# Cross attention's product of probabilities and values: four column positions of 32 x 64 in place of two of 64 x 128

## The chip, the core and the metric

The kernel runs on one core of one Trainium2 chip. The core has TensorE (PE, matmuls), VectorE (DVE), ScalarE (ACT), GpSimd (POOL) and SyncE (SP, which issues the loads here). Each engine works through its own list of instructions and waits on semaphores for the others. What is measured is the device time of one launch in microseconds (us).

## What is computed

One block of a Perceiver: cross attention of 8 x 64 tokens on a context of 8 x 512 rows, a linear attention, and a mixture of 16 experts with a shared expert, each with a layer norm and a residual. The change touches the first of them:

```python
def _L0_xattn_ref(q, k, v, Wq, bq, Wk, bk, Wv, bv, Wo, bo):
    qh = (q @ Wq + bq).reshape(b, n, H, HD)
    kh = (k @ Wk + bk).reshape(b, k.shape[1], H, HD)
    vh = (v @ Wv + bv).reshape(b, v.shape[1], H, HD)
    scores = jnp.einsum('blhe,bshe->bhls', qh, kh)
    attn = jax.nn.softmax(scale * scores, axis=-1)
    out = jnp.einsum('bhls,bshd->blhd', attn, vh)
    out = out.reshape(b, n, H * HD)
    return out @ Wo + bo
...
x = x + _L0_xattn_ref(_layernorm(x, axis=-1), ctx_1024, ctx_1024, ...)
```

For each of the 8 batches and each of the 16 heads, 64 x 512 probabilities are multiplied by 512 x 32 values; the 16 results of 32 columns stand side by side as the 512 rows of the output projection.

## The kernel before

All of it is one program with an order written out by hand. Activations stand transposed (features on partitions). `P` is 128, `B` = 8 batches, `L` = 64 tokens, `HD` = 32, `KT` = `NS` = 4 tiles of 128, `HPT` = 4 heads in a tile, `PAIRS` = 8 pairs of heads. `ps` is PSUM, eight banks of 128 partitions x 512; the bank `AV` (4) takes the attention's output.

The cross attention runs over the batches. PE's step for batch b is `step(b, par)`: keys of b for three tiles (`project_k`, L964), transposes of the first tile of probabilities of batch b-1 (`probs_transpose`, L1037), keys of the last tile, `attention(b-1)`, and then `values_and_scores(b)`: scores of the first two tiles (`score_group`, L1010), two tiles of values (L964), scores of the other two tiles, two tiles of values. After the seventh step `attention(7)` follows alone, and then the output projection (`residual`, L1093), which waits for `o_done`.

`attention(b)` is `probs_transpose(1)`, `attend(0)`, `probs_transpose(2)`, `attend(1)`, `probs_transpose(3)`, `attend(2)`, `attend(3)`. A `probs_transpose(ht)` turns the 512 probabilities of two pairs of heads into two PSUM banks; ACT copies the first (L469), DVE the second (L702), to `probs_T`, and `attend(ht)` waits for both copies (`pT_done`). The next transposes wait for the copies too, since they write the same two banks.

A pair of heads shares 128 rows of `probs`, and so 128 columns of `probs_T`: 64 tokens of one head on one side and 64 of the other on the other side; which head stands on which side alternates with the tile. `attend` (L1047) takes the value columns of both heads of a pair (64) as weights and all 128 columns of `probs_T` as the moving operand. Half of the 64 x 128 result is what is wanted, each head's values by its own tokens, and the other half, each head's values by the other's tokens, is left in the bank. The two pairs of a tile go to the lower and the upper 64 partitions (two column positions of the array).

`o_out` (L710, DVE) picks the wanted blocks out of the bank, for each head of a tile by itself (32 partitions, four blocks of 64), adds the bias of the values and writes `o_T`, whose rows are those of the output projection. It waits for all four attends of a batch (`o_ps`).

DVE's step is: four copies of transposed probabilities (L702), `o_out(b-1)`, `ctx_low(b+1)` (L680, the low part of the next context; it needs ACT's `ctx_high`, L442), and `softmax(b)` (maxima L727, reciprocals L717, scaling L719). ACT's step is: the bias of the keys (L458), its copies of probabilities (L469), `ctx_high(b+1)`, and the exponentials of the scores (L476) with the copies of the values between (L454). PE's second group of scores waits for the third exponential of the first group. In step 7 there is no next context, and `ctx_high` and `ctx_low` are left out.

Matmuls of type fp32 are carried out as two instructions each; a program's list shows one, the trace two.

Of the kernel before, what the change touches and what calls it, by code (L numbers as in the profile page):

```python
# [16 lines left out]
ALU = mybir.AluOpType  # L17
# [3 lines left out]
P = 128  # L21
B, L, S, D = 8, 64, 512, 512
H, HD, FEAT = 16, 32, 128
# [3 lines left out]
KT = D // P  # L27
NS = S // P
NF = FF // P
HPT = P // HD  # L30
# [8 lines left out]
def perceiver_block(nc, x_d, ctx_d, wq_d, bq_d, wk_d, bk_d, wv_d, bv_d, wo_d, bo_d, wqkv_d, proj_d,  # L39
                    wout_d, bout_d, gate_d, wg_d, wu_d, wd_d, wsg_d, wsu_d, wsd_d, out_d):  # L40
    main = ExitStack()
    with main:
# [44 lines left out]
        v_s = sb(cross, "v_s", [P, NS, D])  # L87
# [8 lines left out]
        probs_T = sb(cross, "probs_T", [P, 2, 2, NS, P])  # L96
        o_T = sb(cross, "o_T", [P, KT, TOK])
# [5 lines left out]
        bias_v = sb(cross, "bias_v", [P, KT])  # L103
# [16 lines left out]
        rows = ExitStack()  # L120
# [85 lines left out]
        ps = main.enter_context(nc.psum_tensor("ps", [P, 8, BANK], F32))  # L206

        def bank(n):
            return ps[:, n, :]
# [21 lines left out]
        o_ps, o_done = sem("o_ps"), sem("o_done")  # L231
# [25 lines left out]
        PROJ, TRANS, AV = (0, 1), (2, 3), 4  # L257
# [374 lines left out]
        def _(dve):  # L632
# [71 lines left out]
            def o_out(b):  # L704

                dve.wait_ge(o_ps, b * KT + KT)
                for hh in range(HPT):
                    rows = slice(HD * hh, HD * (hh + 1))
                    blocks = slice(1, 3) if hh % 2 else slice(0, 4, 3)
                    dve.tensor_tensor(o_T[rows, :, bass.ds(b * L, L)].rearrange("p (t u) l -> p t u l", u=2),  # L710
                                      bank(AV).rearrange("p (t c l) -> p t c l", t=2, l=L)[rows, :, blocks, :],
                                      bias_v[rows, :].rearrange("p (t u) -> p t u", u=2).unsqueeze(3).to_broadcast(
                                          [HD, 2, 2, L]), ALU.add).then_inc(o_done, 1)

            def normalise(b, p):
                dve.wait_ge(exp_done, b * PAIRS + p + 1)
# [84 lines left out]
            u = w = a = 0  # L801
            for kind, i, r in LIN_ORDER:
# [24 lines left out]
                else:  # L827
# [4 lines left out]
                    for par in range(2):  # L832
                        ins = dve.tensor_scalar(den[L * par:L * (par + 1), a, :].rearrange("p (k h) -> p k h", k=2),
                                                got[par][:, :, :, HD], 1e-8, None, ALU.add)
                    link(ins)
                    link(dve.reciprocal(den_inv[:, a, :], den[:, a, :]))
                    for par in range(2):
                        rows = slice(L * par, L * (par + 1))
                        ins = dve.tensor_tensor(att[rows, r, 256 * i:256 * (i + 1)].rearrange("p (k h c) -> p k h c", k=2, h=HPT),
                                                got[par][:, :, :, 0:HD],  # L840
                                                den_inv[rows, a, :].rearrange("p (k h) -> p k h", k=2).unsqueeze(3).to_broadcast(
                                                    [L, 2, HPT, HD]), ALU.mult)
# [45 lines left out]
            for b in range(B):  # L888
                ins = dve.max(top_w[:, b, :], score_T[:, L * b:L * (b + 1)])
            link(ins)  # L890
            for b in range(B):
                ins = dve.max_index(top_i[:, b, :], top_w[:, b, :], score_T[:, L * b:L * (b + 1)])
# [13 lines left out]
            for i in range(2):  # L906
                dve.wait_ge(pick_ps, i + 1)
                cols = slice(BANK * i, BANK * (i + 1))
# [40 lines left out]
        def _(pe):  # L949
# [91 lines left out]
            def attend(b, ht):  # L1041
                for pr in range(2):
                    pe.wait_ge(pT_done[pr], b * KT + ht + 1)
                for st in range(NS):
                    for pr in range(2):
                        cols = slice(2 * HD * (2 * ht + pr), 2 * HD * (2 * ht + pr + 1))
                        ins = pe.matmul(ps[64 * pr:64 * (pr + 1), AV, P * ht:P * (ht + 1)], v_s[:, st, cols],  # L1047
                                        probs_T[:, ht % 2, pr, st, :], start=(st == 0), stop=(st == NS - 1),
                                        skip_group_check=True)
                ins.then_inc(o_ps, 1)  # L1050

            def attention(b):
# [16 lines left out]
            for ht in range(KT):  # L1069
                cols = slice(P * ht, P * (ht + 1))  # L1070
                for dt in range(KT):
                    for i, (w, c) in enumerate(((wq_hi, xn_hi), (wq_hi, xn_lo_cross), (wq_lo, xn_hi))):
                        ins = pe.matmul(bank(2 + ht), w[:, dt, cols], c[:, dt, :],  # L1073
                                        start=(dt == 0 and i == 0), stop=(dt == KT - 1 and i == 2))
# [19 lines left out]
                                        start=(dt == 0), stop=(dt == KT - 1))  # L1094
                    ins.then_inc(res_ps, 1)

            pe.wait_ge(o_done, B * HPT)
            pe.wait_ge(wo_in, 16)
            residual(0, o_T, w_o)

# [32 lines left out]
            u = w = a = 0  # L1133
            for kind, i, r in LIN_ORDER:
                if kind == "p":
                    qkv_project(i)
                elif kind in "kq":
# [6 lines left out]
                    if kind == "k":  # L1144
                        for pr in range(2):
                            for part in range(2):
                                ins = pe.matmul(ps[:, u % 3, 2 * FEAT * pr:2 * FEAT * (pr + 1)],
                                                kl_halves[:, i, pr, P * r:P * (r + 1)],
                                                proj_parts[part][:, 2 * i + pr].rearrange("p h f -> p (h f)"),
                                                start=(part == 0), stop=(part == 1))  # L1150
                    else:
                        for part in range(2):
                            ins = pe.matmul(bank(u % 3), proj_parts[part][:, 2 * i + r // 2, r % 2, :],
                                            ql_halves[:, i, r // 2, :], start=(part == 0), stop=(part == 1))
# [14 lines left out]
                else:  # L1169
# [5 lines left out]
                    for h in range(2 * HPT):  # L1175
                        ins = pe.matmul(ps[:, 3 + 2 * (a % 2) + h // HPT, 2 * KVW * (h % HPT):2 * KVW * (h % HPT + 1)],  # L1176
                                        q_feat[:, 8 * i + h, P * r:P * (r + 1)], kv[:, r, 8 * i + h, :],
                                        start=True, stop=True)
# [189 lines left out]
```

## Time and profile before

| what | value |
|---|---|
| timed runs (3) | median 737.51 us, 737.16 to 739.67 |
| profiled execution | 737.64 us |
| its span on the core | 735.9 us |
| mean granted TensorE clock | 0.99 of 2.4 GHz |
| PE busy | 685.9 us, 93% |
| PE weight loads (beside matmuls) | 440.2 us, 60% |
| DVE busy | 302.4 us, 41% |
| ACT busy | 239.7 us, 33% |
| POOL busy | 42.5 us, 6% |
| L1047, matmuls of `attend` | 512 instructions, 33.8 us busy |
| L1037, transposes of probabilities | 256 instructions, 34.1 us busy |
| start of the output projection of the cross attention | 300.1 us of the span |

A span is the time from the first to the last instruction of the program on the core; what lies around it is in the execution's time alone. Busy time of an engine is the time in which at least one of its instructions is under way, so that matmuls that overlap are counted once, while the mean ns of one is its whole length, the way through the array included. An engine's time matters where the others wait for it. The rows further down show this for one step of the cross attention.

### The profile page before, as it was taken

Reading aid. Unit: us, or ns where it says so; the run is one execution under the profiler, and the core shown is the slowest. Engines: PE = TensorE matmul, PEld = TensorE weight load, DVE = VectorE, ACT = ScalarE, POOL = GpSimd, SP = SyncE. Lnnn points to the kernel's source line nnn. Section 1 sums busy time; section 2 is a strip of 40 time slices with the busy share of each in tenths; the row PEclk is TensorE's granted clock in tenths of the full one; section 3 lists DMA queues with packets and bytes.
Section 4 is the critical chain, followed back from the end, with each engine's and each line's share of the span. In section 5 each row is a group of like instructions: output and inputs, shape, how many; then the busy total and the mean of one; then the engine's idle time right before and its main releaser. Section 6 shows DMA issues by size and latency. Waiting matters only on the chain.

```text
span 735.9 us, 9457 instructions
## 1 busy us (share of the span) xinstructions
PE 685.9 (93%) x3760; PEld 440.2 (60%) x3760; DVE 302.4 (41%) x619; ACT 239.7 (33%) x468; POOL 42.5 (6%) x43
## 2 busy tenths in 40 slices
PE   6699999999999999869998989999999999999996
PEld 5468687877768687447897565344444444444532
DVE  4844726445362717576678654111111111111112
ACT  4444434354443525144675122111111111111110
POOL 0800000000000000065000010000000000000000
PEclk9999999999999999989999999999999999999999
DMA  8110101011033000030209740799999999999921
GB/s 302 55 58 1 58 2 57 1 58 55 4 136 151 1 1 1 1 100 24 102 16 419 280 201 1 264 348 376 407 366 412 355 405 356 384 377 380 391 81 60
DMA packets 14344, 129.63 MB, mean 176 GB/s; under 512 B 2720, under 2 KB 2848, under 8 KB 6240
## 3 DMA queue, kind: packets, MB, share of 16 engines
q1 hardware_dynamic: 12384, 127.09, 44.7%
q10 hardware_dynamic: 1920, 1.97, 0.9%
q8 instruction: 30, 0.49, 0.3%
q14 instruction: 10, 0.08, 0.0%
HBM read 126.03 MB, written 1.05 MB: 173 GB/s over the span
## 4 chain that ended last, share of the span: by engine, by line
PE 77%; DVE 13%; ACT 4%; issue 3%; DMA 1%; SPq 1%; ACTq 1%; DVEq 0%
PE ps L964 17%; PE ps L1206 14%; PE ps L1238 8%; PE ps L1213 7%; PE ps L1047 4%; PE ps L1245 4%; PE ps L1127 4%; PE ps L1037 4%; DVE ctx_lo L680 2%; PE ps L1227 2%; PE ps L1164 2%; PE ps L1073 2%; PE ps L1010 1%; PE ps L1176 1%; DVE neg_max L727 1%
## 5 line engine op out<-in xcount | busy, mean ns | idle before, releaser
L860 DVE TENSOR_TENSOR hid<-hid,ps 128x256 f32<-128x256 f32 (+1 forms) x32 | 17.6, 553 | 141.6 <-PE ps L1206 91.8
L702 DVE COPY probs_T<-ps 128x512 f32<-128x512 f32 x32 | 22.1, 692 | 99.9 <-PE ps L1037 99.9
L476 ACT ACTIVATE probs<-ps,neg_max 128x512 f32<-128x512 f32 x64 | 43.8, 687 | 57.1 <-DVE neg_max L727 57.1
L585 ACT ACTIVATE hid<-ps 128x256 f32<-128x256 f32 (+1 forms) x32 | 15.7, 490 | 141.6 <-PE ps L1213 86.5
L1238 PE MATMUL ps<-w_d,hid_T 128*64 128x512 f32 x256 | 58.4, 598 | 1.4 <-ACT hid_T L600 1.4
L1206 PE MATMUL ps<-w_u,x_slot 128*64 128x512 f32 x256 | 58.4, 598 | 0.0
L1206 PE MATMUL ps<-w_g,x_slot 128*64 128x512 f32 x256 | 57.8, 593 | 0.0
L964 PE MATMUL ps<-wv_hi,ctx_hi 128*128 128x512 f32 x128 | 52.5, 410 | 4.1 <-POOL wv_lo L395 4.1
L964 PE MATMUL ps<-wv_lo,ctx_hi 128*128 128x512 f32 x128 | 50.5, 395 | 0.0
L964 PE MATMUL ps<-wv_hi,ctx_lo 128*128 128x512 f32 x128 | 50.5, 394 | 0.0
L964 PE MATMUL ps<-ctx_hi,wk_hi 128*128 128x512 f32 x112 | 44.5, 398 | 0.0
L964 PE MATMUL ps<-ctx_hi,wk_lo 128*128 128x512 f32 x112 | 43.8, 391 | 0.0
L727 DVE TENSOR_REDUCE neg_max<-ps 128x1 f32<-128x512 f32 x64 | 42.5, 684 | 3.2 <-PE ps L1010 3.0
L964 PE MATMUL ps<-ctx_lo,wk_hi 128*128 128x512 f32 x112 | 43.6, 389 | 0.0
L458 ACT ACTIVATE k_T<-ps,bias_k 128x512 f32<-128x512 f32 x32 | 21.8, 688 | 57.0 <-PE ps L964 57.0
L1206 PEld LDWEIGHTS ps<-w_g,x_slot 128*64 128x64 f32 x256 | 18.1, 137 | 37.1 <-issue 37.1
L1238 PEld LDWEIGHTS ps<-w_d,hid_T 128*64 128x64 f32 x256 | 17.0, 136 | 34.1 <-issue 32.3
L964 PEld LDWEIGHTS ps<-wv_hi,ctx_hi 128*128 128x128 f32 x128 | 24.4, 191 | 21.3 <-issue 6.5
L1206 PEld LDWEIGHTS ps<-w_u,x_slot 128*64 128x64 f32 x256 | 17.1, 136 | 30.5 <-issue 30.5
L1037 PE MATMUL ps<-ident,probs 128*128 128x128 f32 x256 | 34.1, 276 | 0.4 <-ACT probs_T L469 0.4
L1047 PE MATMUL ps<-probs_T,v_s 128*64 128x128 f32 x512 | 33.8, 278 | 0.0
L876 DVE TENSOR_TENSOR eo<-ps,eo 64x512 f32<-64x512 f32 x15 | 10.3, 688 | 56.8 <-ACT eo L612 56.8
(192 smaller groups left out, 1167.9 us busy)
## 6 DMA issues: line engine op xcount, KB each, us to landing
w_u<-in_wu SPq DMA_DIRECT2D x16, 2048.0 KB, 16.2
w_d<-in_wd SPq DMA_DIRECT2D x16, 2048.0 KB, 14.7
w_g<-in_wg SPq DMA_DIRECT2D x16, 2048.0 KB, 10.4
ctx_raw<-in_ctx SPq DMA_DIRECT2D x7, 1024.0 KB, 4.8
w_qkv<-in_wqkv SPq DMA_DIRECT2D x1, 3072.0 KB, 13.8
ws_g<-in_wsg SPq DMA_DIRECT2D x1, 2048.0 KB, 7.8
ws_u<-in_wsu SPq DMA_DIRECT2D x1, 2048.0 KB, 7.6
ws_d<-in_wsd SPq DMA_DIRECT2D x1, 2048.0 KB, 22.4
```

What stands on the lines that cost most here:

```text
L458: act.activation(k_T[:, ht, :], bank(FIRST_K + ht if first else PROJ[ht % 2]), ACT.Identity, bias=bias_k[:, ht:ht + 1], scale=1.0).then_in ...
L476: act.activation(probs[:, p, :], bank(SCORE[p]), ACT.Exp, bias=neg_max[:, p:p + 1], scale=1.0, accum_out=row_sum[:, p:p + 1]).then_inc(exp ...
L702: dve.tensor_copy(probs_T[:, ht % 2, 1].rearrange("p s c -> p (s c)"), bank(TRANS[1])).then_inc(pT_done[1], 1)
L727: dve.tensor_reduce(neg_max[:, p:p + 1], bank(SCORE[p]), AX.X, ALU.max, negate=True).then_inc(max_done, 1)
L964: ins = pe.matmul(dst, a(dt), c(dt), start=(dt == 0 and i == 0), stop=(dt == KT - 1 and i == 2))
L1037: ins = pe.transpose(ps[:, TRANS[pr], P * st:P * (st + 1)], probs[:, 2 * ht + pr, P * st:P * (st + 1)], ident[:])
L1047: ins = pe.matmul(ps[64 * pr:64 * (pr + 1), AV, P * ht:P * (ht + 1)], v_s[:, st, cols], probs_T[:, ht % 2, pr, st, :], start=(st == 0), st ...
L1127: ins = pe.matmul(bank(qkv_bank(n)), a, c, start=(dt == 0 and i == 0), stop=(dt == KT - 1 and i == 2))
L1206: ins = pe.matmul(ps[64 * fh:64 * (fh + 1), dst, :], x_slot[:, dt, e, :], weights[e % 2][:, dt, BANK * fh:BANK * (fh + 1)], start=(dt == 0 ...
L1213: ins = pe.matmul(ps[:, dst, 0:w], xn_T[:, dt, P * t:P * (t + 1)], shared[:, dt, f:f + w], start=(dt == 0), stop=(dt == KT - 1))
L1238: ins = pe.matmul(ps[64 * fh:64 * (fh + 1), 6 + n % 2, :], hid_T[:, n % 2, j, 64 * fh:64 * (fh + 1)], w_d[e % 2][:, KT * fh + j, :], start ...
L1245: ins = pe.matmul(bank(6 + n % 2), hid_T[:, n % 2, j, :], ws_d[:, ITEMS[n][2] // P + j, :], start=(j == 0), stop=(j == tiles - 1))
```

## The change

`attend` takes each head by itself. Its weights are the 32 value columns of one head, its moving operand the 64 columns of `probs_T` that are this head's tokens, and its result goes to the 32 partitions `HD * j` of the bank, in columns `L * ht`: four column positions, one for each head of a tile. Nothing is computed that isn't used; the number of multiplied blocks is halved and the number of matmuls doubled. The results of a batch fill half of the bank (256 columns), with rows and tiles as `o_T` has them, and `o_out` becomes one instruction over 128 partitions. PE's wait for `o_done` counts one for each batch.

```diff
--- before.py
+++ after.py
@@ -704,13 +704,9 @@
             def o_out(b):
 
                 dve.wait_ge(o_ps, b * KT + KT)
-                for hh in range(HPT):
-                    rows = slice(HD * hh, HD * (hh + 1))
-                    blocks = slice(1, 3) if hh % 2 else slice(0, 4, 3)
-                    dve.tensor_tensor(o_T[rows, :, bass.ds(b * L, L)].rearrange("p (t u) l -> p t u l", u=2),
-                                      bank(AV).rearrange("p (t c l) -> p t c l", t=2, l=L)[rows, :, blocks, :],
-                                      bias_v[rows, :].rearrange("p (t u) -> p t u", u=2).unsqueeze(3).to_broadcast(
-                                          [HD, 2, 2, L]), ALU.add).then_inc(o_done, 1)
+                dve.tensor_tensor(o_T[:, :, bass.ds(b * L, L)],
+                                  bank(AV)[:, 0:KT * L].rearrange("p (t l) -> p t l", l=L),
+                                  bias_v[:].unsqueeze(2).to_broadcast([P, KT, L]), ALU.add).then_inc(o_done, 1)
 
             def normalise(b, p):
                 dve.wait_ge(exp_done, b * PAIRS + p + 1)
@@ -1042,11 +1038,12 @@
                 for pr in range(2):
                     pe.wait_ge(pT_done[pr], b * KT + ht + 1)
                 for st in range(NS):
-                    for pr in range(2):
-                        cols = slice(2 * HD * (2 * ht + pr), 2 * HD * (2 * ht + pr + 1))
-                        ins = pe.matmul(ps[64 * pr:64 * (pr + 1), AV, P * ht:P * (ht + 1)], v_s[:, st, cols],
-                                        probs_T[:, ht % 2, pr, st, :], start=(st == 0), stop=(st == NS - 1),
-                                        skip_group_check=True)
+                    for j in range(HPT):
+                        pr, side = j // 2, (j + ht) % 2
+                        cols = slice(P * ht + HD * j, P * ht + HD * (j + 1))
+                        ins = pe.matmul(ps[HD * j:HD * (j + 1), AV, L * ht:L * (ht + 1)], v_s[:, st, cols],
+                                        probs_T[:, ht % 2, pr, st, L * side:L * (side + 1)],
+                                        start=(st == 0), stop=(st == NS - 1), skip_group_check=True)
                 ins.then_inc(o_ps, 1)
 
             def attention(b):
@@ -1094,7 +1091,7 @@
                                         start=(dt == 0), stop=(dt == KT - 1))
                     ins.then_inc(res_ps, 1)
 
-            pe.wait_ge(o_done, B * HPT)
+            pe.wait_ge(o_done, B)
             pe.wait_ge(wo_in, 16)
             residual(0, o_T, w_o)
```

On PE, in step 1, around `attention(0)`: `probs_T,v_s` are the matmuls of `attend`, `ident,probs` the transposes, `k_T,q_T` the scores. Before:

```order
L1037 MATMUL ps<-ident,probs 128x128 x8
L1047 MATMUL ps<-probs_T,v_s 64x128 x8
L1037 MATMUL ps<-ident,probs 128x128 x8
L1047 MATMUL ps<-probs_T,v_s 64x128 x8
L1037 MATMUL ps<-ident,probs 128x128 x8
L1047 MATMUL ps<-probs_T,v_s 64x128 x16
L1010 MATMUL ps<-k_T,q_T 64x512 x8
```

After:

```order
L1033 MATMUL ps<-ident,probs 128x128 x8
L1044 MATMUL ps<-probs_T,v_s 32x64 x16
L1033 MATMUL ps<-ident,probs 128x128 x8
L1044 MATMUL ps<-probs_T,v_s 32x64 x16
L1033 MATMUL ps<-ident,probs 128x128 x8
L1044 MATMUL ps<-probs_T,v_s 32x64 x32
L1006 MATMUL ps<-k_T,q_T 64x512 x8
```

The places stay; each block of attend has twice the matmuls, of a quarter of the size.

On DVE, in the loop over the steps, between the last copy of probabilities and the first maxima (ISA and REGISTER_ALU set registers for addresses and waits). Before:

```order
L702 COPY probs_T<-ps 128x512
L706 ISA
L710 ISA
L710 TENSOR_TENSOR o_T<-ps,bias_v 32x4x64
L710 ISA
L710 TENSOR_TENSOR o_T<-ps,bias_v 32x4x64
L710 ISA
L710 TENSOR_TENSOR o_T<-ps,bias_v 32x4x64
L710 ISA
L710 TENSOR_TENSOR o_T<-ps,bias_v 32x4x64
L679 REGISTER_ALU
L680 TENSOR_TENSOR ctx_lo<-ctx_raw,ctx_hi 128x2048
```

After:

```order
L702 COPY probs_T<-ps 128x512
L706 ISA
L707 ISA
L707 TENSOR_TENSOR o_T<-ps,bias_v 128x4x64
L679 REGISTER_ALU
L680 TENSOR_TENSOR ctx_lo<-ctx_raw,ctx_hi 128x2048
```

Three instructions and their address registers are gone; the order of the rest is the same.

## Rows read from the trace of the kernel before

**Rows 1.** The page's chain of work that ended last, shares of the span.
```profile
PE 77%; DVE 13%; ACT 4%; issue 3%; DMA 1%; SPq 1%; ACTq 1%; DVEq 0%
PE ps L964 17%; PE ps L1206 14%; PE ps L1238 8%; PE ps L1213 7%; PE ps L1047 4%; PE ps L1245 4%; PE ps L1127 4%; PE ps L1037 4%; DVE ctx_lo L680 2%; PE ps L1227 2%; PE ps L1164 2%; PE ps L1073 2%; PE ps L1010 1%; PE ps L1176 1%; DVE neg_max L727 1%
```

**Rows 2.** The page's costliest groups: busy us, mean ns, idle before.
```profile
L1047 PE MATMUL ps<-probs_T,v_s 128*64 128x128 f32 x512 | 33.8, 278 | 0.0
```

**Rows 3.** PE's waits over the span: us in total, times, longest.
```profile
PE ps L1010 <- ACT probs L476: 8.1, 6, 1.4
...
PE ps L1316 <- DMA eo_slot<-eo: 1.2, 1, 1.2
```

**Rows 4.** Timeline of a step, all engines: start us, us, engine, line.
```profile
64.05 1.03 PE L1037 MATMUL ps<-ident,probs 128*128 128x128 f32 x8
...
68.45 0.57 ACT L469 COPY probs_T<-ps 128x512 f32<-128x512 f32 x1
...
68.63 1.09 PE L1047 MATMUL ps<-probs_T,v_s 128*64 128x128 f32 x16
68.74 0.69 DVE L702 COPY probs_T<-ps 128x512 f32<-128x512 f32 x1 [2.92 <-PE ps L1037]
...
69.66 1.09 PE L1037 MATMUL ps<-ident,probs 128*128 128x128 f32 x8
...
72.73 2.04 PE L1047 MATMUL ps<-probs_T,v_s 128*64 128x128 f32 x32
72.83 0.69 DVE L702 COPY probs_T<-ps 128x512 f32<-128x512 f32 x1 [1.36 <-PE ps L1037]
72.88 1.90 ACT L442 CAST ctx_hi<-ctx_raw 128x2048 fp32r<-128x2048 f32 x1
...
74.70 1.11 PE L1010 MATMUL ps<-k_T,q_T 32*64 32x512 f32 x16
74.93 1.77 DVE L710 TENSOR_TENSOR o_T<-ps,bias_v 32x256 f32 x4 [1.40 <-PE ps L1047]
...
76.73 2.29 DVE L680 TENSOR_TENSOR ctx_lo<-ctx_raw,ctx_hi 128x2048 fp32r<-128x2048 f32 x1
...
82.50 0.19 ACT L476 ACTIVATION_READ_ACCUMULATOR probs<-ps,neg_max 128x1 f32 x1
...
82.81 0.27 PEld L1010 LDWEIGHTS ps<-k_T,q_T 32*64 32x64 f32 x16 [1.75 <-issue]
82.84 1.12 PE L1010 MATMUL ps<-k_T,q_T 32*64 32x512 f32 x16 [1.36 <-ACT probs L476]
```

**Rows 5.** Timeline of step 7, PE, the two groups of scores.
```profile
276.33 1.11 PE L1010 MATMUL ps<-k_T,q_T 32*64 32x512 f32 x16
...
283.04 1.11 PE L1010 MATMUL ps<-k_T,q_T 32*64 32x512 f32 x16
```

**Rows 6.** DVE's groups by shape: busy us, mean ns, idle before.
```profile
L710 DVE TENSOR_TENSOR o_T<-ps,bias_v 32x256 f32 x24 | 10.1, 421 | 8.9 <-PE ps L1047 8.4
...
L860 DVE TENSOR_TENSOR hid<-hid,ps 128x256 f32<-128x256 f32 x16 | 6.6, 419 | 43.9 <-PE ps L1213 43.9
```

**Rows 7.** Single lines: ns of one instruction, min/median/max.
```profile
L1010 PEld LDWEIGHTS ps<-k_T,q_T x256: 127/130/132, 47.7 to 283.1; 32*64 32x64 f32 x128
L1010 PE MATMUL ps<-k_T,q_T x256: 587/598/638, 47.8 to 283.6; 32*64 32x512 f32 x128
...
L1037 PE MATMUL ps<-ident,probs x256: 270/273/330, 64.1 to 296.0; 128*128 128x128 f32 x128
```

**Rows 8.** Timeline of PE, four heads' keys times values: 96 moving columns.
```profile
371.10 1.03 PE L1164 MATMUL ps<-v_bd,k_feat 128*128 128x96 f32 x8
```

**Rows 9.** Timeline of the last attention's end, DVE and PE.
```profile
298.30 1.77 DVE L710 TENSOR_TENSOR o_T<-ps,bias_v 32x256 f32<-32x256 f32 x4 [1.28 <-PE ps L1047]
...
300.13 3.27 PE L1093 MATMUL ps<-w_o,o_T 128*128 128x512 f32 x7 [1.87 <-DVE o_T L710]
```

**Rows 10.** One stretch: busy (count) of PE, PEld, DVE, ACT, POOL; clock, DMA.
```profile
67.60:82.80 15.20, 13.88 (x129) 10.61 (x127) 9.47 (x16) 6.46 (x12) 0.00 (x0) 1.00 0.16 56
```

## The prediction

> **What bounds the kernel now.** I read the page's chain first, then PE's waits, then the timeline of one batch step, then single lines for prices. The profiled execution took 737.64 us, its span is 735.9 us, and 1.7 us lie around it; the timed runs have a median of 737.51 us, so a sum made against the profile holds for the median within 0.13 us. TensorE (PE) carries 77% of the chain that ended last, VectorE (DVE) 13% [rows 1]. The changed matmuls (L1047) have 4% of it and keep PE busy for 33.8 us [rows 1, 2]. They all lie in the cross attention, which ends with o_T at 300 us [rows 9]; what follows can only be shifted. Loads won't undo the shift: the one wait of PE for a DMA takes 1.2 us and is for a transfer that the kernel itself makes late [rows 3], and the experts' loads are started by work that shifts along.
>
> Seven batch steps and a last attention make up the stage. A step shows three things [rows 4]. First, transposes (eight, L1037) and probabilities times values ("attend", sixteen TensorE instructions, L1047, since each fp32 matmul is carried out as two) take turns with no idle time: an attend from 68.63 to the transposes at 69.66, 1.03 us, and four such blocks up to 72.73. The last two attends stand together, and the scores follow at 74.70. Second, DVE turns to the attention's output only when the last attend has ended: o_T from 74.93 for 1.77 us, ctx_lo for 2.29 up to 79.02, then the row maxima. Third, PE needs exponentials that hang on those maxima and arrives too early: the second group of scores starts at 82.84 after 1.36 us idle. That wait occurs six times and sums to 8.1 us [rows 3]. In step 7, which has no ctx_lo, the way from the first group to the second takes 283.04 - 276.33 = 6.71 us [rows 5] where the others need 82.84 - 74.70 = 8.14 [rows 4]: the stall is worth 1.43 us. So a step has two bounds: PE to the end of attention, then DVE and ScalarE (ACT) up to the second group of scores. The granted clock is 1.00, the level of 2.4 GHz, over both parts, with the stall in it [rows 10]; I expect no change of it.
>
> **DVE: four instructions become one.** Each o_T instruction works on 32 partitions with 256 elements in each and takes 420 ns; the four last 1.77 us [rows 4, 6]. The new one has 128 partitions and the same 256 elements. A sum with a PSUM operand on 128 x 256 takes 419 ns [rows 6]: partitions cost nothing, elements do. I take 0.42 us, a gain of 1.77 - 0.42 = **1.35 us** a batch. The bound above is 1.77, if each group of partitions were paid for, and no gain; the row speaks against it. The wait on o_done counts one a batch in place of four, has the same last event and costs nothing.
>
> **PE: four column positions.** Before, an attend is eight rounds of two instructions, one for each half of the array's columns, with 64 weight columns and 128 tokens. Eight transposes, also with 128 moving columns, take 1.03 us, of which 0.27 are the last one's own: a round is (1.03 - 0.27)/7 = 0.109 us [rows 4, 7]. The attend's sixteen fit in about the same length, so its two halves run side by side and a round of two costs what one matmul costs. The block of 1.03 is 0.05 for the first weights, 7 x 0.109 = 0.76, and 0.21 up to the next block, where the engine changes its tiling.
>
> After, it is eight rounds of four, each with 32 weight columns and 64 moving columns. A round goes with the moving columns: seven instructions with 512 take 3.27 us, about (3.27 - 0.60)/6 = 0.445 us each with the first one's weights in it, four times the 0.109 of 128 [rows 7, 9]. Eight matmuls with 96 moving and 128 weight columns take 1.03 us, as long as transposes with 128 and 128: there the weights are the bound, at about 0.11 [rows 8]. So 32 weight columns cost about 0.027 and 64 moving columns 0.055, and a round costs **0.055 us** if four positions run together. No row shows four. The nearest are the scores (L1010), with eight positions, four of rows by two of columns, and 512 columns: sixteen instructions take 1.11 us, of which 0.59 are the last one's own, so all start within 0.52 us, where sixteen in a row would need some 7 [rows 4, 7, 9]. Nor is issuing the limit: their sixteen weight loads take 0.27 us, less 0.13 for the last, so they start within 0.14 with half of the matmuls between them, 24 instructions at 6 ns [rows 4, 7]. A round of four needs eight instructions, 0.05 us. That is nearly the round itself, so this cover is thin. The bounds: 0.055 by the columns from below, 0.22 from above if four positions take turns; 0.109 if a round keeps its price. I take 0.055, since the row nearest to it, the attend itself, pays nothing for its second column position. The new block: 0.03 + 7 x 0.055 + 0.02 + 0.20 = 0.64 us, **0.39 us** less.
>
> The Trainium skill has a rule against this. Its page "TensorE: Matmul & The Clock Gate", section "Wait — 56ns, not 53.3ns?", says that the starts of two matmuls are never less than some 25 ns apart, however small they are. By it a round of four takes 0.10 us, the attend gains 0.06, and the kernel ends at about 727 us (an estimate from the page's figure). The starts in the scores' rows, 6 ns an instruction, disagree with it where the positions differ.
>
> **What lies on the path.** Four attends a batch, but not each pays. The first two stand between transposes, and these wait for the copies of their banks. The ACT copy ends at 68.45 + 0.57 = 69.02, the DVE copy at 68.74 + 0.69 = 69.43; the next transposes would start at 69.66 - 0.39 = 69.27, and the half that needs the DVE copy about 0.5 us later [rows 4]. Both are in time; the next pair stands alike. The fourth needs the DVE copy of the last transposes, which ends at 72.83 + 0.69 = 73.52; with 0.15 us to be told (as from the third exponential's end at 82.69 to PE's 82.84) that is 73.67. Today the fourth starts at 74.70 - 1.03 = 73.67 [rows 4]. So the 0.39 us of the third turn into a wait for DVE, and the fourth pays again. Attention gains 3 x 0.39 = **1.17 us** a batch.
>
> Steps 1 to 6: PE gains 1.17 + 1.43 = 2.60 up to the second group of scores; the chain over DVE gains 1.17 + 1.35 = 2.52 and stays last by 0.08. What could be late next is ctx_hi, which ctx_lo needs: ACT ends it at 72.88 + 1.90 = 74.78 [rows 4], two attends earlier 74.00, and o_T then ends at 74.93 + 1.77 - 2.52 = 74.18: in time by 0.18. So six steps gain 6 x 2.52 = 15.1 us. Step 7 has no stall to lose: 1.17. The last attention gains 1.17, and PE stands idle through its o_T until 300.13 [rows 9], 1.35 more: 2.52. Sum 15.1 + 1.2 + 2.5 = **18.8 us**: 737.6 - 18.8 = 718.8 us.
>
> **Rivals.** (a) Issuing keeps a round at about 0.082 us, halfway: the attend gains 0.19, a step 0.57 + 1.35 = 1.92, in all 6 x 1.92 + 0.57 + 1.92 = 14.0, so 723.6 us. For it speaks the thin cover. (b) The PE part doesn't do what it says: each matmul keeps its price of 0.109/4 = 27 ns whatever its size, the round stays at 0.109, and DVE alone pays, 7 x 1.35 = 9.5 us: 728.1 us. Against it stand the 6 ns of the scores. The page's 25 ns comes out beside it. (c) Slower: the four positions take turns on the moving side, since four streams of tokens are read from the same 128 partitions, where the scores and the attend read two. A round is 4 x 0.055 = 0.22, an attend grows by 7 x 0.11 = 0.77 us, 32 of them by 24.6, less 9.5 of DVE: 752.7 us. It decides from a round of 0.109 + 9.5/(32 x 7) = 0.151 us, 38 ns a matmul. Against it: the second stream costs nothing today. (d) The third attend pays too: 8 x 0.39 = 3.1 more, 715.7 us. Its copy is tied to the transposes, so little speaks for it.
>
> **How the numbers follow.** Forecast, with (d) as its edge: 0.72; (a) 0.10; (b) 0.10; (c) 0.06; nothing that can be measured 0.02. The time is the forecast's. The range goes from (d), 715.5, to just beyond (a), 724.5; (b), (c) and no change are left out, 0.18. A measurement of this kernel tells about 0.5% (3.7 us) from no change: faster 0.92, same 0.02, slower 0.06.
>
> **What would show it.** L1047's successor should have 1024 instructions and some 21 us busy in place of 33.8; the starts of transposes should follow at 1.66 us in place of 2.05; PE should idle about 0.3 us before the fourth attend; o_T should be eight instructions of 0.42 us; PE's wait for the exponentials should fall from 8.1 us to under 1. I am wrong if an attend block takes over 0.8 us ((a) or (b)) or over 1.03 ((c)), or if ctx_lo starts late behind ctx_hi.

## The result, and the profile after

The changed kernel takes 717.06 us (median of four, 716.97 to 717.97) against 738.59 us of the kernel before in the same comparison (737.16 to 739.73): a ratio of 0.971, 95% interval 0.969 to 0.974. The forecast was 718.8, range 715.5 to 724.5. The profiled execution took 717.97 us, with a span of 716.2 us.

The page's line on the chain that ended last, which answers [rows 1]:

```profile
PE 82%; DVE 10%; ACT 3%; DMA 1%; issue 1%; SPq 1%; ACTq 1%; DVEq 0%
```

The group of the new matmuls among PE's lines (busy us, mean ns of one, idle before them), which answers [rows 2]:

```profile
L1044 PE MATMUL ps<-probs_T,v_s 128*32 128x64 f32 x1024 | 20.9, 222 | 2.3 <-DVE probs_T L702 2.3
```

The product has twice its instructions and 20.9 us busy in place of 33.8. PE's share of the chain rose, DVE's fell. PE's waits, which answer [rows 3] (us in total, times, longest):

```profile
PE ps L1044 <- DVE probs_T L702: 2.3, 8, 0.3
```

The wait for the exponentials is gone from the list; in its place stands one for the copies of the probabilities, eight times 0.29 us. The same step as in [rows 4] (timeline: start us, us, engine, line):

```profile
68.16 0.58 ACT L469 COPY probs_T<-ps 128x512 f32<-128x512 f32 x1
...
68.34 0.65 PE L1044 MATMUL ps<-probs_T,v_s 128*32 128x64 f32 x32
...
68.92 1.09 PE L1033 MATMUL ps<-ident,probs 128*128 128x128 f32 x8
...
71.55 0.65 PE L1044 MATMUL ps<-probs_T,v_s 128*32 128x64 f32 x32
71.66 0.69 DVE L702 COPY probs_T<-ps 128x512 f32<-128x512 f32 x1 [0.91 <-PE ps L1033]
71.70 1.90 ACT L442 CAST ctx_hi<-ctx_raw 128x2048 fp32r<-128x2048 f32 x1
...
72.50 0.65 PE L1044 MATMUL ps<-probs_T,v_s 128*32 128x64 f32 x32 [0.29 <-DVE probs_T L702]
...
73.08 1.11 PE L1006 MATMUL ps<-k_T,q_T 32*64 32x512 f32 x16
73.33 0.42 DVE L707 TENSOR_TENSOR o_T<-ps,bias_v 128x256 f32 x1 [0.98 <-PE ps L1044]
73.67 2.28 DVE L680 TENSOR_TENSOR ctx_lo<-ctx_raw,ctx_hi 128x2048 fp32r<-128x2048 f32 x1
...
79.30 0.19 ACT L476 ACTIVATION_READ_ACCUMULATOR probs<-ps,neg_max 128x1 f32 x1
...
79.80 1.11 PE L1006 MATMUL ps<-k_T,q_T 32*64 32x512 f32 x16
```

An attend has 0.65 us from its first start to its last end, and its block, from 68.34 to the transposes at 68.92, is 0.58 us where it was 1.03. The first two give what they save. The third starts at 71.55, the fourth only at 72.50, since DVE's copy (71.66 + 0.69) has to end first. o_T is one instruction of 0.42 us. The second group of scores starts 79.80 - 73.08 = 6.72 us after the first, as step 7 did all along; it was 8.14. The rest of the step is unchanged, so one step takes 108.32 - 74.70 = 33.6 us before and 103.91 - 73.08 = 30.8 us after. The next step's first scores in the timeline of before:

```profile
108.32 1.11 PE L1010 MATMUL ps<-k_T,q_T 32*64 32x512 f32 x16
```

and in the timeline of after:

```profile
103.91 1.11 PE L1006 MATMUL ps<-k_T,q_T 32*64 32x512 f32 x16
```

And the end of the last attention, which answers [rows 9]:

```profile
278.76 0.42 DVE L707 TENSOR_TENSOR o_T<-ps,bias_v 128x256 f32<-128x256 f32 x1 [0.86 <-PE ps L1044]
...
279.24 3.27 PE L1090 MATMUL ps<-w_o,o_T 128*128 128x512 f32 x7 [0.54 <-DVE o_T L707]
```

From the first scores to the output projection PE takes 300.13 - 47.78 = 252.35 us before and 279.24 - 47.50 = 231.74 after: **20.6 us** less, all of it in the stretch the prediction spoke of. The profiled pair differs by only 19.7 us in its spans. The missing 0.9 us lies in two stretches that the change doesn't touch. Up to the first scores the profile of after is 47.78 - 47.50 = 0.3 us shorter. From the output projection to the experts it is 167.1 - 165.9 = 1.2 us longer, with a mean granted clock of 0.95 in place of 0.97. That stretch, with columns as in [rows 10], before:

```profile
300.10:466.00 165.90, 147.31 (x754) 109.92 (x754) 106.66 (x244) 69.73 (x131) 25.77 (x18) 0.97 0.35 136
```

and after:

```profile
279.20:446.30 167.10, 148.71 (x754) 111.06 (x754) 106.68 (x244) 69.75 (x131) 25.80 (x18) 0.95 0.34 135
```

The profiles of the experiments below show the same spread, whatever was changed: the first scores start between 46.7 and 48.6 us, and from the output projection to the end it takes 435.1 to 437.0 us. So two median times, each of a few runs, can differ by 1 us or more without a cause in the kernel. The length of a step and that of the attention stage, from the first scores to the output projection, are much finer measures, and the readings below rest on them.

### The profile page after: what moved, and what is told of

Same layout as the page of the kernel before. It is cut to its first block, busy times and chain, and to the rows that moved or that the text cites. A ratio compares the mean times of both kernels' runs of the same rounds, so it can differ in the third digit from the quotient of the medians.

```text
span 716.2 us, 10439 instructions
## 1 busy us (share of the span) xinstructions
PE 674.3 (94%) x4272; PEld 429.9 (60%) x4272; DVE 291.3 (41%) x595; ACT 239.9 (33%) x468; POOL 42.6 (6%) x43
## 4 chain that ended last, share of the span: by engine, by line
PE 82%; DVE 10%; ACT 3%; DMA 1%; issue 1%; SPq 1%; ACTq 1%; DVEq 0%
PE ps L960 23%; PE ps L1203 15%; PE ps L1235 8%; PE ps L1210 7%; PE ps L1124 4%; PE ps L1242 4%; PE ps L1033 4%; PE ps L1006 2%; PE ps L1044 2%; PE ps L1224 2%; PE ps L1161 2%; PE ps L1070 2%; PE ps L1173 1%; DMA x<-in_x 1%; DVE stats L642 1%
## 5 line engine op out<-in xcount | busy, mean ns | idle before, releaser
L856 DVE TENSOR_TENSOR hid<-hid,ps 128x256 f32<-128x256 f32 (+1 forms) x32 | 17.6, 554 | 141.6 <-PE ps L1203 91.4
L612 ACT COPY eo<-ps 64x512 f32<-64x512 f32 x15 | 8.7, 580 | 72.4 <-PE ps L1235 72.4
```

The costliest lines, as they stand in the source:

```text
L856: dve.tensor_tensor(hid[:, n % 2, 0:w], hid[:, n % 2, 0:w], ps[:, 2 * (n % 2) + 1, 0:w], ALU.mult).then_inc(hid_done, 1)
```

## The experiments

Each was timed in three or more rounds beside the kernel before. For a step I give the time from one batch's first scores to the next one's, which is the same in steps 1 to 6 within 0.03 us: 33.60 before, 30.83 after. The attention stage takes 252.35 us before and 231.74 after, as above.

### Each part alone

The PE part alone, in the kernel after:

```diff
-                dve.tensor_tensor(o_T[:, :, bass.ds(b * L, L)], ...
+                for hh in range(4):
+                    rows = slice(32 * hh, 32 * (hh + 1))
+                    dve.tensor_tensor(o_T[rows, :, bass.ds(b * L, L)],
+                                      bank(AV)[rows, 0:KT * L].rearrange("p (t l) -> p t l", l=L), ...
-            pe.wait_ge(o_done, B)
+            pe.wait_ge(o_done, B * 4)
```

> The PE part of the change alone: attends in four column positions, but o_T still in four instructions of 32 partitions. Theory (two bounds in a step: PE up to the end of attention, then DVE and ACT up to the second group of scores): attention is 1.35 us shorter a batch, as after the change, and the stall before the second group of scores stays at about 1.4 us in six steps, since PE and DVE's chain both move by the same 1.35. So 8 x 1.35 = 10.8 us under before, about 726.5 us. Rival (the stall is PE's own, and the shorter attends take it away): 718 us, with no wait for the exponentials in the trace.

Measured: 727.17 us (ratio 0.984, 0.982 to 0.986); a step takes 32.28 us. PE's waits:

```profile
PE ps L1008 <- ACT probs L476: 8.2, 6, 1.4
```

The stall of 1.4 us stands there six times as in the kernel before, though PE works less. The theory of two bounds holds, the rival falls.

The DVE part alone, in the kernel before: `o_out` as after the change, attends as before.

> The DVE part alone: attends as before (two column positions of 64 x 128), and one o_T instruction of 128 partitions. It takes the first half of the bank for every partition, so it adds up the wrong blocks of the result: the choice of blocks is what is left out. Theory: the chain over DVE is 1.35 us shorter, and 0.08 more since the next instruction starts before the last one's end; the wait for the exponentials falls from 1.4 us to about 0 in six steps, step 7 gains nothing, the last attention 1.35: 6 x 1.4 + 1.35 = 9.8 us, about 727.6 us. Rival (o_T isn't on the path of a step): only the last 1.35 us, 736 us.

Measured: 727.55 us (0.986, 0.983 to 0.989); a step takes 32.16 us, and PE no longer waits for exponentials. So 1.33 us a step come from PE's part and 1.44 from DVE's, 2.77 together, and the change has 33.60 - 30.83 = 2.77. Over the attention stage (first scores to output projection) it is 10.6 and 10.0 against 20.6. The two parts add up without loss: the first shortens the attention, which PE's way and DVE's way to the second group of scores have in common, and the second shortens DVE's way alone, which was the one that ended last.

### What a round of four costs

Four positions with all 128 columns, in the kernel before:

```diff
-                    for pr in range(2):
-                        cols = slice(2 * HD * (2 * ht + pr), 2 * HD * (2 * ht + pr + 1))
-                        ins = pe.matmul(ps[64 * pr:64 * (pr + 1), AV, P * ht:P * (ht + 1)], v_s[:, st, cols],
-                                        probs_T[:, ht % 2, pr, st, :], ...
+                    for j in range(HPT):
+                        cols = slice(P * ht + HD * j, P * ht + HD * (j + 1))
+                        ins = pe.matmul(ps[HD * j:HD * (j + 1), AV, P * ht:P * (ht + 1)], v_s[:, st, cols],
+                                        probs_T[:, ht % 2, j // 2, st, :], ...
```

> Four column positions with 32 weight columns, but all 128 columns of the transposed probabilities as the moving operand, as before the change; the result lies in the bank as before, and o_T is as before. Twice the instructions of before, the same columns streamed in each position. Theory (a round costs its moving columns, whatever the number of positions): a round of four takes 0.11 us as a round of two did, the block from an attend to the transposes 1.0 us, and the time is that of before, 737.5 us within 1. It also tells whether the shorter change of tiling after the change (0.15 us from the last start to the transposes, 0.20 before) comes from the moving columns: then it is 0.20 here. Rival (each position or each instruction has a price of its own, some 27 ns a matmul and up): 0.11 us or more beside what the columns take, 745 us and up.

Measured: 738.38 us, ratio 0.9997 (0.9986 to 1.0009). Timeline of a step:

```profile
67.54 1.08 PE L1047 MATMUL ps<-probs_T,v_s 128*32 128x128 f32 x32
68.55 1.09 PE L1037 MATMUL ps<-ident,probs 128*128 128x128 f32 x8
...
71.60 2.03 PE L1047 MATMUL ps<-probs_T,v_s 128*32 128x128 f32 x64
```

Twice the instructions, four streams in place of two, and the same time to 0.1%: here the two more positions and the doubled instructions are free, and the columns cost. From the first attend to the transposes it is 1.01 us; without the last matmul's own 0.27 its starts span 0.81, so the change of tiling takes 0.20 us from the last start, as before. After the change it was 0.58 - (0.65 - 0.22) = 0.15. So that time goes with the last matmul's moving columns and not with the number of positions: 64 columns fewer, 0.05 us less.

Half of the columns again, in the kernel after (the diff is `L * ht:L * ht + L // 2` and `L * side:L * side + L // 2` for the ends of the two slices):

> The change with only 32 of the 64 tokens streamed for each head; the other half of the attention's output is left out (the bank's old contents are added up in its place). Four starts of a round lie 7 ns apart in the trace of after, so issuing needs 0.028 us a round, and the columns need 0.028 too. Theory (a round goes with its columns until issuing is reached): round 0.03 us, block from the first attend to the transposes 0.38 us in place of 0.58; three attends a batch pay 0.2, 8 x 3 x 0.2 = 4.8 us: 712.3 us. Rival (a round has a floor near 0.05 us, so 64 columns were already at it): 716 to 717 us.

Measured: 715.92 us (0.969, 0.967 to 0.971), a step 30.44 us, the attention stage 228.71 us. That is 3.0 us less than after (the medians are only 1.1 apart, within their spread), where the theory had 4.8 and the rival next to nothing. Timeline of a step:

```profile
69.30 0.58 ACT L469 COPY probs_T<-ps 128x512 f32<-128x512 f32 x1
...
69.48 0.46 PE L1044 MATMUL ps<-probs_T,v_s 128*32 128x32 f32 x32
...
70.02 1.06 PE L1033 MATMUL ps<-ident,probs 128*128 128x128 f32 x8
70.69 0.58 ACT L469 COPY probs_T<-ps 128x512 f32<-128x512 f32 x1 [0.81 <-PE ps L1033]
...
71.02 0.46 PE L1044 MATMUL ps<-probs_T,v_s 128*32 128x32 f32 x32
...
71.42 1.17 PE L1033 MATMUL ps<-ident,probs 128*128 128x128 f32 x8
```

The round did fall: 32 starts take 0.46 us less the last one's own 0.20, (0.26 - 0.02 - 0.03)/7 = 0.03 us each round, as the theory said, so the rival's floor of 0.05 us isn't there. But the three attends didn't all gain the same. ACT's copies end at 69.30 + 0.58 = 69.88 and 70.69 + 0.58 = 71.27, and the transposes that wait for them start 0.14 and 0.15 us later, at 70.02 and 71.42. The first block is so held at 70.02 - 69.48 = 0.54 us, 0.04 less than after. The second is 71.42 - 71.02 = 0.40, 0.19 less and near the 0.38 expected; the copy and the end of the attend come at about the same time there. The fourth, which has no transposes behind it, takes 73.85 - 73.46 = 0.39. In the kernel after, the first of these copies ends at 68.16 + 0.58 = 68.74 and the transposes start at 68.92: 0.18 us, so it was in time by only some 0.03 us. The second one has more room (after):

```profile
69.61 0.59 ACT L469 COPY probs_T<-ps 128x512 f32<-128x512 f32 x1 [0.88 <-PE ps L1033]
...
70.53 1.09 PE L1033 MATMUL ps<-ident,probs 128*128 128x128 f32 x8
```

It ends at 70.20 and is in time by 70.53 - 70.20 - 0.15 = 0.18 us. So the change took from the first attend nearly all that could be taken; the second could still give 0.18 us.

### The order of the matmuls

The loop over the heads outside, in the kernel after:

```diff
-                for st in range(NS):
-                    for j in range(HPT):
+                for j in range(HPT):
+                    for st in range(NS):
```

> The change, but with the loop over the heads outside the loop over the four tiles of context: each column position gets its eight instructions one behind the other, and then the next position. The same instructions, columns and result. Theory (the gain comes from four positions running side by side, which needs neighbours in the list to have different positions, since matmuls start in order): starts 0.056 us apart inside a position, 4 x 7 x 0.056 = 1.6 us from the first to the last, block 1.8 us in place of 0.58. Against before each attend grows by 0.74 us, 32 of them 24, and DVE's part gives 9.8 back: about 751 us. It is also what the slower rival of the prediction priced. Rival (the engine finds the parallelism by itself, since it pulls weight loads ahead): about 717 us.

Measured: 734.66 us (0.994, 0.992 to 0.996), a step 33.14 us. Timeline:

```profile
67.78 1.39 PE L1044 MATMUL ps<-probs_T,v_s 128*32 128x64 f32 x32
69.11 1.09 PE L1033 MATMUL ps<-ident,probs 128*128 128x128 f32 x8
...
72.47 2.41 PE L1044 MATMUL ps<-probs_T,v_s 128*32 128x64 f32 x64
```

The order is worth 734.7 - 717.1 = 17.6 us (18.4 in the attention stage, which takes 250.18 us here). With it the block is longer than the 1.03 us of before, and what is left of the gain comes from DVE's part. So the list must not hold one position's matmuls eight in a row. But my 751 us was wrong: the block is 1.33 us, not 1.8. The single records show why, though they don't name the position; I tell positions apart by the steady 0.056 us from start to start and by the length of the first. In the first attend one position's matmuls start at 67.780, 67.860, 67.916, 67.972 and 68.028, and the next position's first (243 ns long, as each position's first is) at 68.034, while three of the first position's eight are still to come: they start at 68.084, 68.140 and 68.195. The next two positions begin the same way, at 68.287 and 68.540. So, read like this, matmuls of another position start ahead of up to three that stand before them in the list; that 32 starts fit into 1.18 us, where one after the other at 0.056 would need 1.7, shows the overlap without this reading. The positions overlap for three rounds of eight. The Trainium skill's page "TensorE: Matmul & The Clock Gate", section "The mechanism", says that matmuls start and end strictly in the list's order; for starts in different positions this trace, so read, doesn't agree.

If so, runs of four in one position should cost next to nothing:

```diff
-                for st in range(NS):
-                    for j in range(HPT):
+                for i in range(NS * HPT):
+                        st, j = 2 * (i // 8) + i % 2, i % 8 // 2
```

> The change with another order of the same matmuls: four instructions (two tiles of context) in one column position, then four in the next, and so on, and then the other two tiles. Eight in one position behind one another gave a block of 1.33 us, and there the next position's first matmul started together with the fifth of eight, so three waiting matmuls of one position didn't hold up another position's. Theory (a position keeps up to three waiting matmuls without holding up the list): with four in a row each position starts within some 10 ns of the one before, all run side by side, block 0.6 us, time 717.1 us. Rival (matmuls of different positions overtake each other only by luck or over a fixed time of 0.25 us): block of 0.7 us and more, 720 us and up.

Measured: 718.36 us (0.972, 0.969 to 0.975), a step 30.92 us against 30.83. Timeline:

```profile
69.08 0.69 PE L1044 MATMUL ps<-probs_T,v_s 128*32 128x64 f32 x32
69.71 1.09 PE L1033 MATMUL ps<-ident,probs 128*128 128x128 f32 x8
```

The four positions start within 0.04 us (69.084, 69.097, 69.111, 69.124), and the block is 69.71 - 69.08 = 0.63 us, against 0.58 with single rounds and the 0.7 and more of the rival. That fits three waiting matmuls as the limit. Of the 0.05 us, 0.02 come from these wider first starts (0.02 us in all with single rounds), and about as much from the second half of the list, where the starts lie up to 0.03 us apart. A step is 0.09 us longer than after. What holds the three I can't tell from this.

### What bounds a step now

Two instructions of 64 partitions for o_T, in the kernel after (the diff as in the PE part alone, with 2 and 64):

> The change, but o_T in two instructions of 64 partitions each, so the chain over DVE grows by about 0.44 us a batch and PE does what it does after the change. In the trace of after, the third exponential's end (79.49, and 0.15 to be told) is some 0.16 us ahead of PE's second group of scores (79.80). Theory (after the change the two bounds of a step lie 0.16 us apart, with PE last): a stall of 0.28 us in six steps, and 0.44 at the end: 2.1 us more than after, 719.2 us. Rival (PE has much room to spare and o_T no longer matters in a step): only the 0.44 at the end, 717.5 us.

Measured: 721.8 us (0.978, 0.976 to 0.980), the attention stage 235.73 us, 4.0 more than after where the theory had 2.1. The direction is that of the theory, the size isn't: PE idles 0.44 us before the second group of scores, which starts 0.53 us later after the first (7.26 against 6.72). Timeline of a step:

```profile
73.00 0.88 DVE L709 TENSOR_TENSOR o_T<-ps,bias_v 64x256 f32 x2 [0.98 <-PE ps L1046]
...
73.90 2.29 DVE L680 TENSOR_TENSOR ctx_lo<-ctx_raw,ctx_hi 128x2048 fp32r<-128x2048 f32 x1
...
76.23 1.29 DVE L725 TENSOR_REDUCE neg_max<-ps 128x1 f32<-128x512 f32 x2
...
80.00 1.12 PE L1008 MATMUL ps<-k_T,q_T 32*64 32x512 f32 x16 [0.44 <-ACT probs L476]
```

The maxima of the same step in the kernel after:

```profile
75.87 1.28 DVE L723 TENSOR_REDUCE neg_max<-ps 128x1 f32<-128x512 f32 x2
```

The two chains over DVE, from the start of o_T to the maxima: 76.23 - 73.00 = 3.23 us here and 75.87 - 73.33 = 2.54 after, 0.69 apart where one more instruction is 0.44. The rest is overlap: after, ctx_lo starts 0.08 us before o_T ends and the maxima 0.08 before ctx_lo ends; here both start 0.02 to 0.04 after. It isn't the number of instructions as such: the two maxima, one behind the other, overlap by 0.08 us in every profile. Apart from instructions that need the result of the one ahead, the 0.03 us stand, in all of these profiles, between the pieces of o_T, behind the last piece, and between ctx_lo and the maxima that follow it, and only where o_T comes in pieces of 32 or 64 partitions, of which all but the first start at partition 32, 64 or 96. Whether it is the start or the size of a piece was not tested, and the mechanism stays open. With 0.69 and a stall of 0.53 the chain had about 0.16 us to spare after the change, which is what was read from its trace.

ctx_hi and ctx_lo moved, in the kernel before and in the kernel after:

```diff
 # ACT
                 k_out(b, 0)
+                if more:
+                    ctx_high(b + 1, 1 - par)
                 k_out(b, 1)
...
                 probs_T_out(b - 1, (1, 2, 3))
-                if more:
-                    ctx_high(b + 1, 1 - par)
 # DVE
+                if more:
+                    ctx_low(b + 1, 1 - par)
                 probs_T_out(b - 1)
                 o_out(b - 1)
-                if more:
-                    ctx_low(b + 1, 1 - par)
                 softmax(b)
```

> The kernel before, with nothing of the change, but ctx_hi (ACT) and ctx_lo (DVE) of the next batch are made during the projection of the keys, where both engines idle, in place of between o_T and the maxima. The chain from attention to the second group of scores loses 2.3 us. Theory (a step's stall of 1.43 us is DVE's chain coming late, whatever is taken out of it): the stall goes, 6 x 1.43 = 8.6 us, 728.9 us; it has the same effect on a step as DVE's part of the change. Rival (the stall hangs on something else than the length of the chain): 737.5 us.

Measured: 730.37 us (0.990, 0.987 to 0.992), against 738.39 us of before beside it, so 8.0 us less. The attention stage takes 243.51 us, 8.8 less than before (8.6 expected). A step takes 32.13 us, as with DVE's part of the change (32.16), and the way from the first to the second group of scores 6.71 us. So the stall is the late chain: it goes when o_T is shortened and also when ctx_hi and ctx_lo are moved. The number of 728.9 was made against a lower time of before.

> The change, with ctx_hi and ctx_lo of the next batch made during the projection of the keys, as in the run on before. Theory (after the change PE alone sets the steps, and the chain over DVE, ctx_hi's end at 73.60 in it, is just in time): nothing to gain, 717.0 us within 0.7. Rival (ctx_hi, which ended 0.07 us ahead of ctx_lo, has become a bound): up to 0.3 us in six steps, 715.5 us.

Measured: 717.02 us (0.971, 0.969 to 0.973), a step 30.83 us and the attention stage 231.78: nothing, as the theory says. After the change PE alone sets a step, and ctx_hi was not a bound.

On top of it, the last copy in two halves:

```diff
 # DVE, probs_T_out: the last tile in two parts
+                    for part in range(2 if ht == KT - 1 else 1):
+                        st = slice(2 * part, 2 * part + 2) if ht == KT - 1 else slice(0, NS)
+                        src = ps[:, SCORE[0], 0:2 * P] if part else ps[:, TRANS[1], P * st.start:P * st.stop]
+                        dve.wait_ge(pT_ps, b * (PAIRS + 1) + 2 * ht + 2 + part)
+                        dve.tensor_copy(probs_T[:, ht % 2, 1, st].rearrange("p s c -> p (s c)"),
+                                        src).then_inc(pT_done[1], 1)
 # PE, probs_transpose: its last two transposes into another bank
+                        apart = ht == KT - 1 and pr == 1 and st >= 2
+                        at = (SCORE[0], st - 2) if apart else (TRANS[pr], st)
...
 # PE, attend
+                    if ht == KT - 1 and st == 2:
+                        pe.wait_ge(pT_done[1], b * (KT + 1) + KT + 1)
```

> On top of the one before: the last two transposes of a batch go to a PSUM bank of their own, and DVE copies the last tile in two halves, the first as soon as its transposes are done. PE's fourth attend starts on the first half and waits for the second half before its third tile of context. Theory (the 0.39 us that the third attend saves are lost to the wait for this copy, 2.3 us idle in eight waits of 0.29, plus the weights that aren't loaded ahead): the fourth attend starts up to 0.44 us sooner, some 0.4 a batch, 8 x 0.4 = 3.2 us: 713.8 us. Rival (the wait is hidden by something else, or the additional waits and the second copy cost what they give): 716 to 717 us.

Measured: 714.11 us (713.86 to 714.53; ratio 0.967, 0.965 to 0.970), a step 30.34 us. Timeline:

```profile
71.18 0.58 ACT L469 COPY probs_T<-ps 128x512 f32<-128x512 f32 x1 [1.02 <-PE ps L1039]
71.40 0.76 DVE L705 COPY probs_T<-ps 128x256 f32<-128x256 f32 x2 [0.69 <-PE ps L1039]
...
71.51 1.13 PE L1053 MATMUL ps<-probs_T,v_s 128*32 128x64 f32 x64
...
72.57 1.11 PE L1010 MATMUL ps<-k_T,q_T 32*64 32x512 f32 x16
```

The copy takes 0.76 us in its halves, more than the 0.69 in one, but starts 0.1 us before the third attend, and the third and fourth attend run as one block of 64 instructions, 1.13 us. Each step is 0.49 us shorter (0.4 expected), and the attention stage, 227.87 us, 3.9 us; the medians are 2.9 apart, and the 713.8 us expected were met. This version is faster than both kernels. So it was this wait that took the third attend's saving.

## Why the prediction was right

The time lies in the range, and 1.7 us under the forecast. The closeness is in part luck: the forecast's gain was 18.8 us, the attention stage gained 20.6, and the medians of the comparison lie 738.59 - 717.06 = 21.5 us apart. The kernel before took 1.1 us more in that comparison than the 737.51 the forecast started from, which hid as much of the shortfall. The mechanism was right, and two terms of it were too small. By its steps:

- **Two bounds in a step.** Right, and shown by taking each part alone and by moving ctx_lo: the stall was DVE's chain, worth 8.14 - 6.72 = 1.42 us (forecast 1.43).
- **DVE's part.** 1.77 to 0.42 us, as forecast. The chain gained some 0.2 us more than that (from o_T's start to the maxima 79.06 - 74.93 = 4.13 us before and 2.54 after), from the next two instructions, which start 0.08 us before the one ahead ends where they stood 0.03 behind it. So the chain, which the sum held to be last by 0.08 us, was ahead by 0.16, and PE's whole gain counted: a step gained 2.77 us in place of 2.52. The maxima of the same step before:

```profile
79.06 1.29 DVE L727 TENSOR_REDUCE neg_max<-ps 128x1 f32<-128x512 f32 x2
```

- **A round of four.** Forecast 0.055 us, measured (0.65 - 0.22 - 0.02 - 0.03)/7 = 0.054 (whole length, less the last matmul's own 0.22, less the forecast's 0.02 and 0.03 for the spread in a round and the first weights); single starts lie 0.056 apart. The doubt about issuing was unfounded: in the records the four of a round start 7 ns apart with a weight load each between, so 3.5 ns an instruction and not 6; the 6 ns had the start of the first ones in it. The Trainium skill's 25 ns between starts ("TensorE: Matmul & The Clock Gate", section "Wait — 56ns, not 53.3ns?") don't hold between positions in this trace; the section doesn't speak of positions, and to apply it to them was the prediction's reading.
- **The block.** The mis-sized term: 0.64 forecast, 0.58 measured; the starts of the transposes follow at 70.53 - 68.92 = 1.61 us (1.66 forecast). I had left the time from the last start to the transposes at 0.20 us; it falls with the moving columns to 0.15. So three attends gave 1.35 us a batch in place of 1.17.
- **The third attend doesn't pay.** Right: the fourth starts 0.95 us after the third (0.94 forecast), after 0.29 us idle (0.3).
- **ctx_hi in time.** Right: it ends at 71.70 + 1.90 = 73.60, 0.15 us before o_T does (0.18 forecast) and 0.07 before ctx_lo starts, and moving it changed nothing.
- **The copies ahead of the next transposes.** In time, as forecast, but the ACT copy that the transposes behind the first attend wait for by only 0.03 us. The prediction set its end (69.02) against the transposes' start (69.27) without the 0.15 us to be told that it used elsewhere; with them its own numbers leave 0.10.
- **The sum.** Six steps 16.6 us (15.1), step 7 1.37 (1.2), the last attention 17.09 - 14.44 = 2.65 (2.5), together 20.6 us (18.8). The terms that fell short are the change of tiling, 8 x 3 x 0.05 = 1.2 us, and, for most of the rest, the overlap on DVE: without it a step would have gained 1.35 + 1.35 = 2.70 us and not 2.77, six times 0.07 us.
- **Rivals.** (a) and (b) fall with the round of 0.056; (c) with that and with the four streams of 128 columns, which cost nothing; (d) with the idle time before the fourth attend, which only the split copy took away.

## What to carry to other kernels

In this kernel four column positions cost what two did, as long as their instructions alternate in the list (four in a row cost 0.09 us a step, eight in a row 2.3); what a round costs is its moving columns. So a product that throws half of its result away can be cut into positions that compute just what is wanted. Find for each shortened block the copy or load that the next block waits for: here the first attend could give 0.45 us and hardly more, and the third gave none until its copy was split. And where a second engine's chain comes last, shorten both; half of this change's gain is one DVE instruction in place of four, which a layout that fits the next stage made possible.

## What the runs showed of the hardware that was not expected

- Matmuls of another column position start ahead of up to three earlier ones that wait in their own position (positions told apart by the spacing of the starts): eight in a row in each of four positions take 1.33 us a block, four in a row 0.63, alternating 0.58.
- From a matmul's start to the first one with another tiling it is 0.20 us with 128 moving columns and 0.15 with 64, where the same tiling goes on after 0.109 and 0.056.
- With 32 columns a round of four positions takes about 0.03 us, so four fp32 instructions with their weight loads can start in that time.
- On DVE an instruction that waits for nothing started 0.08 us before the end of the one ahead (the maxima in every profile, ctx_lo behind a single o_T), but 0.03 us after it between and behind pieces of o_T of 32 or 64 partitions.
